# Issuing a tile's six band reads inside stage A, each behind its own image write, instead of at the start of stage B1

## What is computed

```python
qs = jnp.einsum('bhnd,od->bhno', q, scale_embed)
for i, o in enumerate(OFFSETS):
    qk = jnp.einsum('bhnd,bhnd->bhn', q, _shift(k, o))
    lg = qk * inv * (1.0 + qs[..., i]) + pos_bias[i][None, :, None]
    lg = jnp.where(pos[None, None, :] >= o, lg, NEG)
    logits.append(lg)
p = jax.nn.softmax(jnp.stack(logits, axis=-1), axis=-1)
for i, o in enumerate(OFFSETS):
    out = out + p[..., i][..., None] * _shift(v, o)
gate = jax.nn.sigmoid(x @ gate_w.T + gate_b)
attn = (out * if_gain) * gate @ out_w.T + out_b
x = x + layernorm(attn);  x = x + layernorm(ffn(layernorm(x)))
```

## Time and profile before

| | |
|---|---|
| median of two runs | 3037.62 us (3037.04 to 3038.21) |
| profiled execution | 3048.84 us, span of its slowest core 3047.3 us |
| spans of the eight cores | 3009.8 to 3047.3 us |
| attention stage (first to last rbuf copy) | 888 to 2246 us of the span |

### The profile page before, as it was taken

One profiled execution on the slowest core, in us unless ns is written; L12 is line 12 of the kernel. 1 busy time (PEld: TensorE's weight loads), 2 busy tenths in 40 slices (PEclk: granted clock), 3 DMA queues, 4 the chain that ended last, 5 costly groups with the idle time before them and its releaser, 6 DMA issues.

```text
span 3047.3 us, 18335 instructions; the slowest of 8 cores (3009.8 to 3047.3 us)
## 1 busy us (share of the span) xinstructions
PE 807.4 (26%) x4872; PEld 378.4 (12%) x4872; DVE 1038.0 (34%) x1142; ACT 864.6 (28%) x952; POOL 317.7 (10%) x267
## 2 busy tenths in 40 slices
PE   0139766556410111111111111111111710001620
PEld 0114322222210000000000000000000300001310
DVE  1430110000025454555444455444453043233133
ACT  1543221112124222333322233322231331003333
POOL 1100000000001011111011111011112000210000
PEclk9999998668655555555555555555555855555765
DMA  2322112223222222222222222222224032002023
GB/s 70 104 69 22 14 11 31 54 54 60 71 106 53 67 60 66 66 61 64 46 66 60 63 60 63 51 56 64 65 57 107 24 124 85 5 11 69 28 98 123
DMA packets 396198, 184.97 MB, mean 61 GB/s; under 512 B 342880, under 2 KB 354160, under 8 KB 396096
## 3 DMA queue, kind: packets, MB, share of 16 engines
q10 hardware_dynamic: 205696, 68.63, 9.9%
q1 hardware_dynamic: 147568, 82.54, 8.6%
q0 software_dynamic: 42832, 32.64, 6.0%
HBM read 111.73 MB, written 78.32 MB: 62 GB/s over the span
## 4 chain that ended last, share of the span: by engine, by line
DMA 30%; DVE 23%; ACT 16%; PE 16%; issue 7%; ACTq 5%; SPq 1%; POOL 1%; DVEq 1%; POOLq 0%
PE kqps L325 8%; DVE rbuf L538 6%; DMA rimg<-rbuf 5%; ACT rbuf L539 5%; ACTq L591 4%; DMA psp_img<-Pb 3%; DVE bandx L573 3%; DMA qtok<-qts 2%; DVE scr L570 2%; DMA accTb<-acch 2%; PE opps L757 2%; PE fps L904 2%; DMA ktok<-wcol 2%; DMA q_img<-qtmp 2%; DMA xt<-xs 1%
## 5 line engine op out<-in xcount | busy, mean ns | idle before, releaser
L523 PE MATMUL genps<-kfm,qsl 64*128 64x160 f16 (+2 forms) x768 | 92.7, 337 | 1191.1 <-DMA qtb<-qtok 703.2
L325 PE MATMUL kqps<-y1fm,wcol 128*128 128x512 f16 x1408 | 375.2, 424 | 52.4 <-ACT qtmp L367 29.9
L538 DVE CAST rbuf<-genps 128x640 f16<-128x640 f32 (+2 forms) x96 | 331.8, 3456 | 138.9 <-DMA rimg<-rbuf 111.9
L539 ACT CAST rbuf<-genps 128x640 f16<-128x640 f32 (+2 forms) x96 | 331.9, 3458 | 142.6 <-DMA psp_img<-Pb 68.1
L523 PEld LDWEIGHTS genps<-kfm,qsl 64*128 64x128 f16 x768 | 40.3, 115 | 1257.7 <-issue 1257.6
L325 PEld LDWEIGHTS kqps<-y1fm,wcol 128*128 128x128 f16 x1408 | 145.0, 107 | 237.9 <-issue 123.3
L604 ACT ACTIVATE t2b<-t2b 128x736 f32<-128x736 f32 x16 | 13.1, 816 | 554.4 <-DVE t2b L601 554.4
L667 POOL TENSOR_TENSOR acch<-vtok,Pb 128x1024 f16<-128x1024 f16 x16 | 30.4, 1900 | 1066.3 <-DMA rimg<-rbuf 734.2
L489 DVE TENSOR_TENSOR outfl<-outfl,accTb 128x128 f16<-128x128 f16 x128 | 37.6, 294 | 269.8 <-DMA psp_img<-Pb 134.6
L476 PE MATMUL pvps<-pspsb,vtok 128*64 128x128 f16 x384 | 112.2, 413 | 54.5 <-DMA band<-rimg 37.9
L358 DVE COPY vtok<-trpv 128x512 f16<-128x512 f16 x56 | 23.8, 424 | 272.4 <-PE trpv L352 272.4
(11 more groups left out here) (122 smaller groups left out, 1516.4 us busy)
## 6 DMA issues: line engine op xcount, KB each, us to landing
pspsb<-psp_img ACTq DMA_DIRECT2D x48, 512.0 KB, 5.4
x1r<-x_img ACTq DMA_DIRECT2D x32, 512.0 KB, 3.3
xt<-xs POOLq DMA_DIRECT2D x28, 512.0 KB, 4.0
rimg<-rbuf SPq DMA_DIRECT2D x32, 416.0 KB, 2.5
rimg<-rbuf SPq DMA_DIRECT2D x32, 384.0 KB, 2.7
rimg<-rbuf SPq DMA_DIRECT2D x32, 320.0 KB, 2.3
xres<-xs ACTq DMA_DIRECT2D x16, 512.0 KB, 3.7
x_img<-x1t SPq DMA_DIRECT2D x16, 512.0 KB, 2.6
```

What stands on the lines that cost most here:

```text
L325: e.matmul(_o, _s, _m, start=_st, stop=_sp),
L523: e.matmul(_o, _s, _m, start=True, stop=True, tile_position=_tp), waits, ("TS", 1))
L538: cpf = (lambda e, _o=pout, _i=pin: e.tensor_copy(_o, _i)) if eng == "vector" else \
L539: (lambda e, _o=pout, _i=pin: e.copy(_o, _i))
```

## The change

The six reads R0 to R5 are no longer built in `stage_B1(qt)` but in `stage_A(qt)`, each directly after the image write with its own rwidx. Their addresses, named waits and batch are unchanged. `stage_B1` only collects their tokens.

```diff
@@ stage_A, after each write of rimg
                     rw_tok[(qt, rwidx)] = rw
+                    if gi == 0:
+                        src = bass.AP(t[f"rimg{gi}"], roff, [[8 * w + 16, 128], [1, 33 * 8]])
+                        dst = bass.AP(band[slot][:].tensor, half * 8, [[CW, 128], [16, 33], [1, 8]])
+                    else:
+                        _, _, sb_, ns, ds = GROUPS[gi]
+                        src = bass.AP(t[f"rimg{gi}"], roff, [[8 * w + 16, 128], [8 * ds, ns], [1, 8]])
+                        dst = bass.AP(band[slot][:].tensor, sb_ * 16 + half * 8, [[CW, 128], [16, ns], [1, 8]])
+                    brd_tok[(qt, rwidx)] = S("scalar", lambda e, _o=dst, _i=src: e.dma_start(out=_o, in_=_i),
+                                             (rw, band_used.get(qt - 2)), ("AQ", 16), batch=("brd", qt))
                     rwidx += 1
@@ stage_B1
         slot = qt % 2
-        brd = []
-        rwidx = 0
-        for gi, (w0o, w, sb_, ns, ds) in enumerate(GROUPS):
-            for half in range(2):
-                (the same source and destination as above)
-                brd.append(S("scalar", lambda e, _o=dst, _i=src: e.dma_start(out=_o, in_=_i),
-                             (rw_tok[(qt, rwidx)], band_used.get(qt - 2)), ("AQ", 16), batch=("brd", qt)))
-                brd_tok[(qt, rwidx)] = brd[-1]
-                rwidx += 1
+        brd = [brd_tok[(qt, i)] for i in range(2 * NG)]
```

## The result

The changed kernel took 3287.39 us in the median (3282.92 to 3335.06, eleven runs) against 3040.27 for the kernel before in ten runs. The ratio is 1.081, with an interval of 1.077 to 1.085: slower by 8%, some 247 us. The forecast was 3341 us, 303 more than before. The direction, the place and the terms held; the loss came out a fifth smaller. In a few executions of every kernel one die has a lower granted clock and the cores on it take longer; the ratios leave such executions out, and rows from one are taken on the other die.

The account below looks back on a forecast made before the run. Kernel taken as bound by latency, by waits standing one behind the other. Per steady tile 30.6 + 3.5 - 15.1 = +19.0 us, 14 tiles +266, first two +25 and +12: 3037.6 + 303 = 3341 us, range 3280 to 3430.

Parts of the forecast that it names:

- TensorE and L570 wait for the reads: Attention stage: matmuls and first far-offset multiplication would wait for reads built before them, though they use none of their data.
- The first rival: Matmuls and L570 don't wait; reads only delay ScalarE's stage C copies, 7.2 us a tile: 2912 us, 4 in 100.
- The rounds: Stage A, W0 to W5: image write, read, matmuls and copies become one line, costing 30.6 us more a tile.
- the front: Start of a tile's softmax: reads go out earlier, L612 then bound by the transpose; 15.1 us gained a tile.
- the first two tiles: Tiles 0 and 1, without stage C: +25 and +12 us.
- The third rival: Reads as slow apart as together, 6.1 and 3.9 instead of 4.8 and 2.4 us: 3431 us, 12 in 100.
- Behind the rounds: After the last rbuf copy: first L570 waits 5.2 us for W5 and R5, 1.7 given back at L681; net 3.5.
- SBUF: two separate sides: Tile front: shared port pair could block GpSimd's addition for a whole L597; gain then 14.6, sum 8 us higher.
- Anatomy of one DMA: R0's landing: 2.2 us by the skill against the row's 5.0; by the skill the whole would cost 83 us less.
- The sum: A steady tile: 30.6 + 3.5 - 15.1 = +19.0 us; 14 of them +266, total +303.
- The clock: Attention stage: clock at 0.5, the lower of two levels, so a TensorE with more idle time loses nothing.

Follow-up runs that it names:

- the first experiment: Changed kernel with four waits (stage A and stage C matmuls, first far-offset multiplication, image writes) pinned to their own loads' counts; 2920.56 us, ratio 0.957 to before.
- fifth experiment: Kernel with the six reads at the end of stage A, but with them built before the far-offset loop, not after it; 2978.68 us, ratio 0.982 to before.
- The third experiment: Changed kernel with only the first far-offset multiplication, L579, pinned to the qtb load; 3233.89 us, ratio 1.060 to before.

## Why the prediction was right, step by step

- *TensorE and L570 wait for the reads*: right, 80 and 16 waits, and the first and fifth experiment show that nothing but the count makes them. The first rival (only ScalarE pays, 2912 us) was wrong for the changed kernel, and with the waits pinned its figure was met within 9 us: 2921.
- *The rounds*: 30.6 us forecast, 27.6 measured (63.8 against 36.2). This is where most of the missing 56 us lie: 3.0 x 14 tiles = 42; the next step has 7 more, the front 4, the first two tiles 4. In means of the fourteen tiles the 3.0 close: the five reads took 14.4 us and not 16.8 (medians 4.0 for R0 and R1, 2.1 for R2 and R3, 1.8 for R4, where 4.8 and 2.4 were taken), -2.4; the writes W0 to W4, taken as landing alike in both kernels, landed in 12.5 us together after and 13.8 before, -1.3; the line of instructions and hand-overs was 36.6 and not 35.5, +1.1; what stands beside the landings before was 22.1 and not 21.7, since the tile used had a W4 of 4.76 us, -0.4. The first read of a tile, 5.0 us with R1 right behind it, was no measure of a read that stands apart. Two terms of the line are 0.03 and 0.06 above what their own rows give (6.62 and 6.29), which changes nothing. The third rival (as slow apart as together) went the wrong way.
- *Behind the rounds*: 3.5 forecast. L579 waits 5.07 in the tile shown; L672 and L676 take 2.46 together instead of 4.36 before. From the end of the rbuf copies (1557.2) to the end of L677 (1577.4) it is 20.2 us against 17.4 before: 2.8. The mean of fourteen tiles is 3.0. The third experiment, in which that wait goes and the 2.95 us return, gives 3.5.
- *The front*: 15.1 forecast, 14.9 measured in the tiles shown and 15.4 in the mean, by a reason that was half wrong. The step said that L612 would wait for the transpose by about 1 us and that GpSimd's addition might be held by VectorE. In the trace GpSimd starts first (1577.54) and VectorE's L592 takes 2.65 instead of 0.93, while L681 keeps its 2.13. VectorE's own line is longer by 1.7 and ends about where the transpose lands (L607 waited for it 1.0 us in all, in two tiles). The two errors cancel, which is luck: this term's size is right, its working only in part.
- *By the Trainium skill* (SBUF — State Buffer, section "SBUF: two separate sides") whichever of the two starts first holds the shared port pair for its whole instruction, a VectorE instruction with two SBUF inputs against a GpSimd one that reads SBUF among them. The trace agrees: the later one, here VectorE, lost 1.72 us.
- *By the Trainium skill* (DMA: Bandwidth & Descriptors, section "Anatomy of one DMA") R0 was an estimate of 2.2 us; the section gives its figures for DMAs issued by GpSimd, and these are issued by ScalarE. It landed in 4.0; 128 x 33 pieces of 16 bytes are not priced by their bytes. The small ones, at 1.8 and 2.1, lie near the Trainium skill's fixed 2.0.
- *The sum*: 19.0 a steady tile, 15.2 measured (27.6 + 3.0 - 15.4); the first two tiles +25 and +12, +22 and +10 measured from W0 to W0 (88.6 and 92.7 after, 66.3 and 82.3 before).
- *The clock* stayed at its lower level in the stage, 0.50 in any stretch looked at, before and after.

## What to carry to other kernels

Where a wait on a DMA means a count of everything built so far on a queue, an operation's place in build order is part of every later wait on that queue: before moving a DMA earlier, list who takes a count on its semaphore behind the new place, not who needs its data. The cure is a semaphore per purpose or a pinned count: the same reads in the same place cost 8% with the shared count, gain 4% with it pinned, and are part of a kernel that is 14% faster without it. Most of the gain needs no such cure, only a place ahead of the transpose at the tile boundary: with the reads at the end of stage A a tile takes 76.1 us, with the early place, SyncE's queue and pinned counts 74.4. Price a many-piece DMA from a row where it runs alone, and a wait removed from one engine by what that engine then runs into.

## What was not expected of the hardware

- A read of 128 x 33 pieces of 16 bytes lands in 4.0 us when the other engines wait for it, in 4.7 and 4.4 (R0 and R1, means of the first experiment) when the next image write may go out meanwhile, and in 4.9 and 7.4 (medians) as the first and second of six issued together; one of 128 x 2 pieces in 1.8 apart and 2.4 in the group. Issued together, the second and third read took 2.4 to 4.8 us of ScalarE's queue each (medians 3.2 and 3.1); issued apart, 0.37 to 0.38.
- With GpSimd running, VectorE's product of two SBUF operands (128x736) took 2.65 us instead of 0.93, and one of 128x1024 took 2.95 instead of 1.23: nearly all that was left of GpSimd's instruction was added, so a shift of one engine by 3 us can take away half of the wait that caused it.
